# Gathering the lower expert outputs of a decoder layer in four groups, each behind one more down product

## The chip, the cores and the metric

One core of a Trainium2 chip runs the whole program. The metric is the device time of one execution in microseconds (us), median of several executions; less is better.

## What is computed

A decoder layer on x of shape 4 x 512 x 256 (2048 tokens): a Mamba mixer, cross attention over a context of 1601 positions, and a feed-forward part in which each token goes to two of eight experts. Only the last part is touched:

```python
scores = xt @ Wg.T
topk_scores, topk_idx = jax.lax.top_k(scores, TOP_K)          # TOP_K = 2
gate = jax.nn.silu(jnp.einsum('td,ehd->teh', xt, W1))
up = jnp.einsum('td,ehd->teh', xt, W2)
y = jnp.einsum('teh,edh->ted', gate * up, W3)
out = jnp.einsum('te,ted->td', w, y)                          # w: the two scores, zero elsewhere
return x + out
```

## The kernel before, in words

`decoder_kernel` calls `mixer_phase` (mixer and attention, everything up to about 731 us of the trace) and then `routed_ffn_phase`. All of the order there is written out by hand, engine by engine, with semaphores.

**Sorting.** The 4096 pairs of token and expert are sorted by expert, each expert's part padded to whole tiles of 128 rows. NT = 39 tiles are always computed, numbered 0 to 38; the last ones may be padding. GpSimd (POOL) gathers the token rows of all 39 tiles by indirect DMA (L1224).

**The tile loop.** For a tile, TensorE (PE) transposes the tokens (L1522), computes gate and up products (L1535), transposes the hidden rows (L1544, L1548) and computes the down product (L1559), whose last matmul raises `y_mm` by one: `y_mm` of n means that down products 0 to n - 1 are done. ScalarE (ACT) rounds tokens and hidden rows (L1266, L1277 to L1280) and does the silu (L1272). VectorE (DVE) takes the rests (L1427, L1435), multiplies (L1421), and copies the down product to SBUF (`evacuate`, L1442, the copy to `y_sb`). SyncE (SP) stores `y_sb` to `ffn_sorted` in DRAM (L1153, semaphores `y_st0` for even tiles and `y_st1` for odd ones) and fetches the tokens of the tile four ahead (L1148). PE, ACT and DVE run tiles two by two in a hardware loop, up to tile 36 of gate and up, and then a straight tail.

**Combining.** Each token has two result rows in `ffn_sorted`. The lower one belongs to the expert with the smaller number, so it is never in the last expert's tiles. POOL does, one after the other:

1. `stored(0)`: waits until all tiles of experts 0 to 6 are stored (L1245, L1206).
2. `fetch(y_one, 0, ...)`: 16 indirect gathers of 128 rows of 1 KB, the lower rows (L1239, semaphore `low_ld`).
3. It waits for all sixteen, and for the first 8 of the 16 groups of tokens multiplies by the score and adds to `x_all` (L1254, L1257).
4. `stored(1)`: waits until all tiles of all experts are stored.
5. `fetch(y_two, 1, ...)`: 16 gathers of the upper rows (L1239; `y_two` is part of the buffer `tok`), semaphore `up_ld[g // 2]` for each two.

DVE, in its tail, waits for `low_ld` behind the hidden rests of tile 38, adds the lower rows of the other 8 groups (L1477), copies the down product of tile 38, and then adds the upper rows for all 16 groups (L1487), each two as their gathers land. SP writes `out`, two groups at a time (L1176), waits for the last of it, and the program ends.

The small multiplications at L1206 (`take_wait`) only make POOL's waits take effect. The lines that the prediction speaks of are L1206, L1239, L1254, L1257, L1442, L1477, L1487 and L1176; those of POOL's second half:

```python
stored(0)
fetch(y_one, 0, lambda g: low_ld)
pool.wait_ge(low_ld, 16 * G)
...
stored(1)
fetch(y_two, 1, lambda g: up_ld[g // 2])
```

Of the kernel before, what the change touches and what calls it, by code (L numbers as in the profile page):

```python
# [20 lines left out]
def at(i, n=1):  # L21
    return bass.ds(i, n)
# [985 lines left out]
def routed_ffn_phase(nc, io, dims, env, sem, buf):  # L1008
# [5 lines left out]
    KD, G, KH, H_LAST, HH, NT = (env[k] for k in ("KD", "G", "KH", "H_LAST", "HH", "NT"))  # L1014
# [8 lines left out]
    with ExitStack() as ctx:  # L1023
        def sb(name, shape, dt=F32):
            return buf(ctx, name, shape, dt)
# [49 lines left out]
        y_one = sb("y_one", [P, G, D])  # L1075
        y_two = tok[:, 0:G, :]
# [29 lines left out]
        def so_far(i, p):  # L1106
# [3 lines left out]
        x_mm, xT_hi, xT_lo, gu_mm, silu2_ok, hid_ok, h_mm, hT_hi, hT_lo, y_mm, y_ok2 = (  # L1110
            sem(n) for n in ("x_mm", "xT_hi", "xT_lo", "gu_mm", "silu2_ok", "hid_ok", "h_mm", "hT_hi", "hT_lo", "y_mm",
                             "y_ok2"))
        low_ld, up_ld, comb = sem("low_ld"), [sem(f"up_ld{g}") for g in range(G // 2)], sem("comb")
# [14 lines left out]
        def gathered(i):  # L1128

            return 32 * (i // (2 * PAIRS) + 1) - (16 if i == NT - 1 and NT % 2 else 0)  # L1130

        def reload(eng, e, p, done):

            eng.wait_ge(w_ok, 2 * e + 2)
            load_expert(eng, e + 2, p, done)

        with nc.Block() as block:

            @block.sync
            def _(sp):  # L1140
                load_expert(sp, 0, 0, first_ld[0])
                load_expert(sp, 1, 1, first_ld[1])

                def load(i, q):

                    come = gathered(i) if isinstance(i, int) else (i - q) * (16 // PAIRS) + 32
                    sp.wait_ge(tok_ld[q // 2], come)
                    sp.dma_start(tok_in[:, q % 2, :], tok[:, at(i), :].rearrange("p a d -> p (a d)")  # L1148
                                 ).then_inc(tile_ld[q % 2], 16)

                def store(i, p):
                    sp.wait_ge(y_ok2, i + 1)
                    sp.dma_start(ffn_sorted[at(i * P, P), :], y_sb[:, p, :]).then_inc(y_st[p], 16)  # L1153

                for e in range(2):
                    reload(sp, e, e, first_ld[e])

                def store_and_load(i, q):


                    store(i, q % 2)
                    load(i + AHEAD, (q + AHEAD) % GROUP)

                GROUP = 2 * PAIRS
                LAST = (NT - AHEAD) // GROUP * GROUP
                with sp.Fori(0, LAST // GROUP) as j:
                    for q in range(GROUP):
                        store_and_load(GROUP * j + q, q)
                for i in range(LAST, NT - AHEAD):
                    store_and_load(i, i % GROUP)  # L1170
                for i in range(NT - AHEAD, NT):
                    store(i, i % 2)
                out = io["out"].rearrange("(g p) d -> p g d", p=P)
                for g in range(0, G, 2):
                    sp.wait_ge(comb, g + 2)
                    sp.dma_start(out[:, g:g + 2, :], x_all[:, g:g + 2, :]).then_inc(out_st, 16)  # L1176
                sp.wait_ge(out_st, 16 * (G // 2))

            @block.gpsimd
            def _(pool):  # L1180
                nc.gpsimd.iota(iot[:], pattern=[[1, P]], base=0, channel_multiplier=0).then_inc(iota_ok, 1)
                nc.gpsimd.iota(num[:], pattern=[[P, G]], base=0, channel_multiplier=1).then_inc(iota_ok, 1)
                nc.gpsimd.memset(tri[:], 1.0).then_inc(tri_zero, 1)
                nc.gpsimd.memset(ones[:], 1.0).then_inc(one_ok, 1)
                nc.gpsimd.memset(seg[:], 1.0).then_inc(one_ok, 1)
                pool.wait_ge(one_ok, 2)
                nc.gpsimd.memset(seg[:, :, 0:1], 0.0).then_inc(one_ok, 1)

                pool.wait_ge(tri_zero, 1)
                nc.gpsimd.affine_select(out=tri[:], in_=tri[:], compare_op=ALU.is_gt, fill=0.0, base=0,  # L1190
                                        pattern=[[1, P]], channel_multiplier=-1).then_inc(tri_ok, 1)
                def split(e, p):

                    for n, (lo, hi) in enumerate(PARTS):
                        nc.gpsimd.tensor_copy(w_hi[:, p * NW + lo:p * NW + hi], w_raw[:, p, lo:hi]).then_inc(hi_ok, 1)
                        pool.wait_ge(hi_ok, 2 * e + n + 1)
                        take_wait()
                        nc.gpsimd.tensor_tensor(w_lo[:, p * NW + lo:p * NW + hi], w_raw[:, p, lo:hi],
                                                w_hi[:, p * NW + lo:p * NW + hi].bitcast(F32), ALU.subtract).then_inc(w_ok, 1)

                taken = [0]

                def take_wait():

                    k = taken[0] % 16
                    nc.gpsimd.tensor_tensor(pool_scrap2[:, k:k + 1], ident[:, 0:1], ident[:, 0:1], ALU.mult)  # L1206
                    taken[0] += 1

                def next_expert(e, p, loaded, count):

                    last_tile = pool.value_load(tile_end[0:1, at(e - 2)], min_val=1, max_val=NT)
                    pool.wait_ge(y_mm, last_tile)
                    take_wait()
                    pool.wait_ge(loaded, count)
                    take_wait()
                    split(e, p)


                pool.wait_ge(id_ok, 1)
                for i in range(NT):  # L1220

                    if i % 2 == 0 and i >= 2 * PAIRS:
                        pool.wait_ge(tok_ld[i // 2 % PAIRS], gathered(i - 2 * PAIRS))
                    pool.indirect_dma_start(tok[:, i, :], None, xn3_dram,  # L1224
                                            bass.IndirectOffsetOnAxis(ap=tok_id[:, i:i + 1], axis=0)
                                            ).then_inc(tok_ld[i // 2 % PAIRS], 16)
                pool.wait_ge(tab_ok, 1)
                for p in range(2):
                    next_expert(2 + p, p, first_ld[p], 128)
                    reload(pool, 2 + p, p, wts_ld[p])  # L1230
                with pool.Fori(2, E // 2 - 1) as j:
                    for p in range(2):
                        next_expert(2 * j + p, p, wts_ld[p], 64 * (j - 1))
                        reload(pool, 2 * j + p, p, wts_ld[p])
                for p in range(2):
                    next_expert(E - 2 + p, p, wts_ld[p], 64 * (E // 2 - 2))
                def fetch(y, k, done):
                    for g in range(G):
                        pool.indirect_dma_start(y[:, g, :], None, ffn_sorted,  # L1239
                                                bass.IndirectOffsetOnAxis(ap=pos[:, k, g:g + 1], axis=0)).then_inc(done(g), 16)  # L1240

                def stored(n):

                    for p in range(2):
                        stores = pool.value_load(tile_end[0:1, E + 2 * p + n:E + 2 * p + n + 1], min_val=1, max_val=NT)  # L1245
                        pool.wait_ge(y_st[p], stores * 16)
                        take_wait()

                pool.wait_ge(pos_ok2, 1)
                stored(0)  # L1250
                fetch(y_one, 0, lambda g: low_ld)
                pool.wait_ge(low_ld, 16 * G)
                for g in range(BY_POOL):
                    nc.gpsimd.tensor_scalar(y_one[:, g, :], y_one[:, g, :], w_low[:, 0, g:g + 1], None,  # L1254
                                            ALU.mult).then_inc(low_part, 1)
                    pool.wait_ge(low_part, g + 1)
                    nc.gpsimd.tensor_tensor(x_all[:, g, :], x_all[:, g, :], y_one[:, g, :], ALU.add).then_inc(low_in, 1)  # L1257
                stored(1)
                fetch(y_two, 1, lambda g: up_ld[g // 2])

            @block.scalar
            def _(act):
# [376 lines left out]
```

## Time and profile before

| | us |
|---|---|
| median of three runs | 1065.64 |
| lowest and highest of them | 1062.32, 1066.44 |
| span of the profiled execution (first to last instruction) | 1119.2 |
| PE busy | 908.4 (81%) |
| DVE busy | 670.0 (60%) |
| POOL busy | 599.3 (54%) |
| ACT busy | 446.0 (40%) |

The three runs were timed without the profiler. The execution that the profiler recorded is another one, and its own time is known only as the span. An engine's busy time counts its data instructions alone. A row of the timeline gives the start, the duration, the engine, the line, the operation, and in brackets how long the engine sat idle before it and what ended that: a DMA, another engine's instruction, "issue" (nothing that the profile shows) or "remote" (a releaser that the profile does not know).

### The profile page before, as it was taken

The page shows a single profiled execution, that of the slowest core. Times are in us where ns is not written, and L with a number is a line of the kernel's source. Part 1 is how long each engine was busy: PE and PEld are TensorE (multiplying, and loading weights), DVE is VectorE, ACT ScalarE, POOL GpSimd, SP SyncE. Part 2 cuts the span into 40 slices and gives each one's busy share as a digit, 9 for nine tenths or more (in the row PEclk, how much of TensorE's full clock was granted, in tenths as well). Part 3 has the DMA queues.
Part 4 walks back from the last instruction along what each step waited for, and adds up shares of the span by engine and source line. Part 5 has one row for each costly group of instructions (what it writes and reads, how often), then busy time and mean ns, then how long its engine had stood idle before and what let it go on. Part 6 is the DMA issues. An engine that isn't in the chain of part 4 may idle for free. (4 is left out here: it accounts for less than half of the span.)

```text
span 1119.2 us, 16281 instructions
## 1 busy us (share of the span) xinstructions
PE 908.4 (81%) x5148; PEld 723.8 (65%) x5149; DVE 670.0 (60%) x1091; ACT 446.0 (40%) x827; POOL 599.3 (54%) x499
## 2 busy tenths in 40 slices
PE   5767667899969999788998779736279999999665
PEld 2344345576856677665677647735279999999564
DVE  5188789887789877876878433275034444443215
ACT  2555754467554476543555112231023333332111
POOL 2157785866666676658777132007743466425750
PEclk9989887999969999988999589957589999999686
DMA  9450020000170000530003100045513332212222
GB/s 321 157 199 1 2 113 38 1 15 1 40 264 1 16 1 2 199 103 7 9 1 110 42 7 8 20 155 191 146 39 115 115 115 75 78 37 70 61 89 90
DMA packets 48955, 85.45 MB, mean 76 GB/s; under 512 B 6292, under 2 KB 38696, under 8 KB 46856
## 3 DMA queue, kind: packets, MB, share of 16 engines
q1 hardware_dynamic: 43032, 65.77, 17.4%
q0 software_dynamic: 5872, 19.02, 5.6%
q8 instruction: 29, 0.48, 0.2%
q14 instruction: 22, 0.18, 0.1%
HBM read 65.64 MB, written 14.55 MB: 72 GB/s over the span
## 5 line engine op out<-in xcount | busy, mean ns | idle before, releaser
L413 POOL TENSOR_TENSOR u<-dtx,b_all 128x512 f32<-128x512 f32 x256 | 324.9, 1281 | 176.6 <-DVE h L662 172.9
L662 DVE TENSOR_TENSOR_SCAN h<-da,u 128x512 f32<-128x512 f32 x256 | 307.5, 1215 | 55.8 <-ACT da L497 33.9
L497 ACT ACTIVATE da<-dt_,a_neg 128x512 f32<-128x512 f32 x256 | 174.5, 690 | 105.9 <-DVE h L662 105.2
L785 PEld LDWEIGHTS ysum<-ident,h 128*128 128x128 f32 x1024 | 128.4, 152 | 94.5 <-DVE h L662 45.0
L785 PE MATMUL ysum<-ident,h 128*128 128x128 f32 x1024 | 157.7, 293 | 32.5 <-DVE h L662 25.5
L1421 DVE TENSOR_TENSOR hid<-act_,ps_u 128x352 f32<-128x352 f32 x78 | 40.4, 521 | 134.7 <-ACT act_ L1272 128.4
L965 PE MATMUL pv<-pT,ctx_n 128*128 128x128 f32 (+1 forms) x832 | 104.6, 276 | 1.4 <-DVE x_all L722 1.3
L965 PEld LDWEIGHTS pv<-pT,ctx_n 128*128 128x128 f32 (+1 forms) x832 | 98.4, 192 | 6.5 <-DVE x_all L722 3.2
L936 PE MATMUL pa<-ctx_t,xnT_a 128*128 128x401 f32 (+1 forms) x256 | 94.2, 502 | 3.6 <-ACT xnT_a L548 1.8
L1272 ACT ACTIVATE act_<-ps_g 128x352 f32<-128x352 f32 x78 | 36.1, 465 | 149.9 <-PE ps_u L1535 92.6
L1559 PE MATMUL ps_y<-w_hi,hidT_hi 128*128 x234 | 68.1, 291 | 19.0 <-issue 15.0
L1559 PE MATMUL ps_y<-w_hi,hidT_lo 128*128 x234 | 68.1, 291 | 15.2 <-issue 15.2
L1559 PE MATMUL ps_y<-w_lo,hidT_hi 128*128 x234 | 68.1, 291 | 13.1 <-issue 13.1
L768 PE MATMUL pm<-xnT_m,w_in 128*128 128x512 f32 x128 | 68.8, 645 | 10.2 <-DVE xs L619 5.3
L1206 POOL TENSOR_TENSOR pool_scrap<-ident 128x1 f32<-128x1 f32 x28 | 5.1, 192 | 121.8 <-PE ps_y L1559 103.5
L774 PE MATMUL pm<-xs,w_dt 128*128 128x512 f32 x128 | 65.8, 622 | 5.2 <-DVE xs L619 4.5
L1435 DVE TENSOR_TENSOR hidT_lo<-ps_h,hidT_hi 128x512 fp32r<-128x512 f32 (+2 forms) x117 | 42.1, 415 | 41.1 <-ACT hidT_hi L1277 29.6
L936 PEld LDWEIGHTS pa<-ctx_t,xnT_a 128*128 128x128 f32 x256 | 45.2, 190 | 33.0 <-DVE sim L645 4.8
L1277 ACT CAST hidT_hi<-ps_h 128x512 fp32r<-128x512 f32 x39 | 22.9, 587 | 102.7 <-PE ps_h L1548 82.0
L645 DVE COPY_PREDICATED sim<-mask,pa 128x401 f32<-128x401 uint8 x64 | 38.3, 600 | 42.4 <-PE pa L936 41.3
L1224 POOL DMA_INDIRECT tok<-xn_dram,tok_id x39 | 43.8, 1124 | 35.7 <-DVE tok_id L1403 24.2
L1559 PEld LDWEIGHTS ps_y<-w_hi,hidT_hi 128*128 128x128 f32 x234 | 46.2, 197 | 22.0 <-issue 22.0
(217 smaller groups left out, 1796.4 us busy)
## 6 DMA issues: line engine op xcount, KB each, us to landing
b_all<-b_dram SPq DMA_DIRECT2D x16, 1024.0 KB, 4.7
ctx_t<-in_ctxT SPq DMA_DIRECT2D x4, 1601.0 KB
ctx_n<-in_ctx SPq DMA_DIRECT2D x4, 1536.0 KB
ffn_sorted<-yg SPq DMA_DIRECT2D x1, 4992.0 KB, 22.5
ffn_sorted<-y_sb SPq DMA_DIRECT2D x39, 128.0 KB
tok_in<-tok SPq DMA_DIRECT2D x35, 128.0 KB
mask<-in_mask SPq DMA_DIRECT2D x16, 200.1 KB, 2.4
w_raw<-in_w1T SPq DMA_DIRECT2D x4, 704.0 KB
```

The costliest lines, as they stand in the source:

```text
L413: nc.gpsimd.tensor_tensor(u[:, i % 2, :], dtx[:, j % 2, :], b_all[:, n, :], ALU.mult).then_inc(u_ok, 1)
L497: nc.scalar.activation(da[i % DS][:], dt_[:, j % 2, :], ACT.Exp, scale=a_neg[:, j, n:n + 1]).then_inc(da_ok, 1)
L662: nc.vector.tensor_tensor_scan(h[:, i % HS, :], da[i % DS][:], u[:, i % 2, :], 0.0, ALU.mult, ALU.add).then_inc(scan_ok, 1)
L768: last = nc.tensor.matmul(bank[:], w_in[:, k, j * P:(j + 1) * P], xnT_m[:, k, :], start=k == 0, stop=k == KD - 1)
L774: last = nc.tensor.matmul(DT_BANKS[j][:], w_dt[:, k, j * P:(j + 1) * P], of_row(xs, b, k), start=k == 0, stop=k == KI - 1)
L785: last = nc.tensor.matmul(ysum[:, t * P:(t + 1) * P], h[:, i % HS, t * P:(t + 1) * P], ident[:], is_transpose=True, start=n == 0 and t == ...
L936: last = nc.tensor.matmul(pa[c % 2][:, 0:hi - lo], xnT_a[:, k, q * P:(q + 1) * P], ctx_t[:, k, lo:hi], start=k == 0, stop=k == KD - 1)
L965: last = nc.tensor.matmul(pv[:, k * P:(k + 1) * P], ctx_n[0:w, c, k * P:(k + 1) * P], pT[0:w, c, :], start=c == 0 and k == 0, stop=c == KC ...
L1224: pool.indirect_dma_start(tok[:, i, :], None, xn3_dram, bass.IndirectOffsetOnAxis(ap=tok_id[:, i:i + 1], axis=0)).then_inc(tok_ld[i // 2 % ...
L1421: nc.vector.tensor_tensor(hid[:, p, c * HH:(c + 1) * HH], act_[:, c * HH:(c + 1) * HH], ps_u[c][:, 0:HH], ALU.mult).then_inc(hid_ok, 1)
L1435: nc.vector.tensor_tensor(hidT_lo[0:rows_in, c:c + n, :], bank[0:rows_in, col:col + n * P].rearrange("p (c m) -> p c m", m=P), hidT_hi[0:r ...
L1559: last = nc.tensor.matmul(ps_y[:, 0:D], x[:, c, :], w[:, at(e % 2 * NW + (2 * NGU + c * D), D)], start=c == 0 and n == 0, stop=c == KH - 1 ...
```

## The change

Ahead of gathers 0, 4, 8 and 12 of the lower rows POOL now waits for one more down product: `y_mm` of at least 32, 33, 34 and 35. The upper gathers are issued as before. `stored(0)` stays ahead of the first.

```diff
-                def fetch(y, k, done):
+                def fetch(y, k, done, spread):
                     for g in range(G):
+                        if spread and g % 4 == 0:
+                            pool.wait_ge(y_mm, NT - 7 + g // 4)
                         pool.indirect_dma_start(y[:, g, :], None, ffn_sorted,
                                                 bass.IndirectOffsetOnAxis(ap=pos[:, k, g:g + 1], axis=0)).then_inc(done(g), 16)
...
-                fetch(y_one, 0, lambda g: low_ld)
+                fetch(y_one, 0, lambda g: low_ld, True)
...
-                fetch(y_two, 1, lambda g: up_ld[g // 2])
+                fetch(y_two, 1, lambda g: up_ld[g // 2], False)
```

POOL before, from the second half of `stored(0)` to the first multiplication (`y_one` receives the lower rows, `pos` has their places):

```order
L1206 TENSOR_TENSOR pool_scrap<-ident 128x1 [waits y_st0]
L1245 TENSOR_LOAD tile_end
L1245 ISA x2
L1246 REGISTER_ALU
L1206 TENSOR_TENSOR pool_scrap<-ident 128x1 [waits y_st1]
L1239 DMA y_one<-ffn_sorted,pos 128x256 x16
L1254 TENSOR_SCALAR y_one<-y_one,w_low 128x256 [waits low_ld]
```

The same place in the changed kernel:

```order
L1206 TENSOR_TENSOR pool_scrap<-ident 128x1 [waits y_st1]
L1241 DMA y_one<-ffn_sorted,pos 128x256 [waits y_mm]
L1241 DMA y_one<-ffn_sorted,pos 128x256 x3
L1241 DMA y_one<-ffn_sorted,pos 128x256 [waits y_mm]
L1241 DMA y_one<-ffn_sorted,pos 128x256 x3
L1241 DMA y_one<-ffn_sorted,pos 128x256 [waits y_mm]
L1241 DMA y_one<-ffn_sorted,pos 128x256 x3
L1241 DMA y_one<-ffn_sorted,pos 128x256 [waits y_mm]
L1241 DMA y_one<-ffn_sorted,pos 128x256 x3
L1256 TENSOR_SCALAR y_one<-y_one,w_low 128x256 [waits low_ld]
```

The run of sixteen gathers now has four waits on `y_mm` in it; no other instruction moved. What stands behind the lower rows' additions on POOL, in the changed kernel (`tok` is the buffer of the upper rows):

```order
L1256 TENSOR_SCALAR y_one<-y_one,w_low 128x256
L1259 TENSOR_TENSOR x_all<-x_all,y_one 128x256 [waits low_part]
L1247 TENSOR_LOAD tile_end
L1247 ISA x2
L1248 REGISTER_ALU
L1206 TENSOR_TENSOR pool_scrap<-ident 128x1 [waits y_st0]
L1247 TENSOR_LOAD tile_end
L1247 ISA x2
L1248 REGISTER_ALU
L1206 TENSOR_TENSOR pool_scrap<-ident 128x1 [waits y_st1]
L1241 DMA tok<-ffn_sorted,pos 128x256 x16
```

This is as before but for line numbers: the upper gathers stand behind all that POOL does with the lower rows.

## Rows read from the trace of the kernel before

**Rows 1.** The core's span and mean granted TensorE clock.

```profile
core 0: 1119.2 us, clock 0.887
```

**Rows 2.** Timeline of DVE, the copies of down products (start us, duration, instruction, idle before).

```profile
781.48 0.42 DVE L1442 COPY y_sb<-ps_y 128x256 f32<-128x256 f32 x1 [1.99 <-PE ps_y L1559]
...
827.39 0.42 DVE L1442 COPY y_sb<-ps_y 128x256 f32<-128x256 f32 x1 [1.26 <-PE ps_y L1559]
...
1014.67 0.42 DVE L1442 COPY y_sb<-ps_y 128x256 f32<-128x256 f32 x1 [1.25 <-PE ps_y L1559]
...
1028.54 0.42 DVE L1442 COPY y_sb<-ps_y 128x256 f32<-128x256 f32 x1 [1.25 <-PE ps_y L1559]
...
1059.35 0.42 DVE L1442 COPY y_sb<-ps_y 128x256 f32<-128x256 f32 x1 [1.25 <-PE ps_y L1559]
...
1066.27 0.42 DVE L1442 COPY y_sb<-ps_y 128x256 f32<-128x256 f32 x1 [1.25 <-PE ps_y L1559]
...
1073.13 0.42 DVE L1442 COPY y_sb<-ps_y 128x256 f32<-128x256 f32 x1 [1.25 <-PE ps_y L1559]
...
1103.32 0.42 DVE L1442 COPY y_sb<-ps_y 128x256 f32<-128x256 f32 x1 [1.13 <-PE ps_y L1559]
...
1109.89 0.42 DVE L1442 COPY y_sb<-ps_y 128x256 f32<-128x256 f32 x1 [1.05 <-PE ps_y L1559]
```

**Rows 3.** Timeline of POOL: last token gather, then the combining.

```profile
811.03 0.95 POOL L1224 DMA_INDIRECT tok<-xn_dram,tok_id  x1 [0.30 <-issue]
...
1024.04 0.19 POOL L1206 TENSOR_TENSOR pool_scrap<-ident 128x1 f32<-128x1 f32 x1 [8.89 <-DMA ffn_sorted<-y_sb]
...
1025.40 1.04 POOL L1239 DMA_INDIRECT y_one<-ffn_sorted,pos  x1 [0.52 <-issue]
1026.74 0.96 POOL L1239 DMA_INDIRECT y_one<-ffn_sorted,pos  x1 [0.30 <-issue]
...
1029.26 0.95 POOL L1239 DMA_INDIRECT y_one<-ffn_sorted,pos  x1 [0.30 <-issue]
...
1044.30 0.95 POOL L1239 DMA_INDIRECT y_one<-ffn_sorted,pos  x1 [0.30 <-issue]
1047.12 0.93 POOL L1254 TENSOR_SCALAR y_one<-y_one,w_low 128x256 f32<-128x256 f32 x1 [1.88 <-DMA y_one<-ffn_sorted,pos]
...
1060.18 0.74 POOL L1257 TENSOR_TENSOR x_all<-x_all,y_one 128x256 f32<-128x256 f32 x1
1068.48 0.19 POOL L1206 TENSOR_TENSOR pool_scrap<-ident 128x1 f32<-128x1 f32 x1 [7.56 <-DMA ffn_sorted<-y_sb]
...
1069.85 1.03 POOL L1239 DMA_INDIRECT tok<-ffn_sorted,pos  x1 [0.54 <-issue]
...
1088.75 0.95 POOL L1239 DMA_INDIRECT tok<-ffn_sorted,pos  x1 [0.30 <-issue]
```

**Rows 4.** Timeline of ACT around the long idle stretches.

```profile
816.12 0.46 ACT L1272 ACTIVATE act_<-ps_g 128x352 f32<-128x352 f32 x1 [25.61 <-remote]
...
1032.58 0.59 ACT L1277 CAST hidT_hi<-ps_h 128x512 fp32r<-128x512 f32 x1 [5.84 <-remote]
...
1034.10 0.37 ACT L1266 CAST tokT_hi<-ps_x 128x256 fp32r<-128x256 f32 x1 [0.62 <-remote]
1048.26 0.82 ACT L1272 ACTIVATE act_<-ps_g 128x352 f32<-128x352 f32 x2 [13.78 <-remote]
...
1092.70 0.82 ACT L1272 ACTIVATE act_<-ps_g 128x352 f32<-128x352 f32 x2 [13.82 <-remote]
```

**Rows 5.** Timeline of PE's weight loads in one such stretch.

```profile
1039.71 0.29 PEld L1559 LDWEIGHTS ps_y<-w_hi,hidT_lo 128*128 128x128 f32 x1 [1.13 <-issue]
```

**Rows 6.** Busy time by stretch: us, then PE, PEld, DVE, ACT, POOL; PEclk; DMA share; GB/s.

```profile
985.00:1028.00 43.00, 43.00 (x315) 42.87 (x314) 17.79 (x43) 12.83 (x37) 16.65 (x12) 1.00 0.12 40
1028.00:1049.00 21.00, 9.94 (x54) 8.53 (x52) 2.08 (x6) 2.02 (x6) 15.07 (x17) 0.73 0.36 106
```

**Rows 7.** Last piece of the chain that ended last: DVE's additions of upper rows.

```profile
1112.69 3.96 DVE x_all L1487 x10
```

## The prediction

> **What bounds the kernel now.** I read the span first [rows 1], then the copies of down products on DVE as a clock of the tile loop [rows 2], then POOL [rows 3], and then what ACT and PE did where the clock stopped [rows 4 to 6].
>
> The last copy is tile 38's (1109.89), the one ahead tile 37's (1103.32); tiles 36, 32 and 30 have no row here, so counting back, 1073.13 is tile 35, 1066.27 tile 34, 1059.35 tile 33, 1028.54 tile 31 and 1014.67 tile 29. Tiles 29 to 31 take 13.87 us, 6.93 us a tile, and in that stretch PE is busy for 43.00 of 43.00 us [rows 6]: the tile loop is TensorE's own speed. There are three places where it is not: tiles 0 to 2 take 45.91 us (781.48 to 827.39) where two tiles are 13.86, tiles 31 to 33 take 30.81, and tiles 35 to 37 take 30.19. They lose 32.0, 16.9 and 16.3 us. Each lies beside a long run of indirect gathers on POOL [rows 3]: the token gathers up to 811.98, the sixteen lower ones (1025.40 to 1045.25), the sixteen upper ones (1069.85 to 1089.70). ACT sits idle 25.61, 13.78 and 13.82 us for a releaser that the profile doesn't know, and goes on 4.1, 3.0 and 3.0 us after the last gather's issue [rows 3, 4]. PE issues one weight load in 1.4 us (1.13 idle plus 0.29) with "issue" ahead of it [rows 5], at a DMA share of only 0.36 [rows 6]. The clock falls to a mean of 0.73 there, between its two levels of 1.2 and 2.4 GHz, after PE had gone nearly idle.
>
> Read alone, this says: gathers stop the other engines, so spread them. But the timed runs say otherwise. The profiled span is 1119.2 us and the runs take 1065.64: **the recorded execution is at least 53.6 us longer than a timed one**, more if a time holds something around the span. The loop's other stretches run at PE's full speed and can't shrink by that. The three stalls can. So I take them for something that happens when the gathers' DMAs and the instructions are recorded together, and absent from the timed runs. The Trainium skill, page "NOTIFIC — the notification-queue block", section 7.1, says that a full internal pipeline of the recording block pushes back on whoever writes records and so can throttle an engine; the long span agrees with this, though no row names the block.
>
> **Before, with the stalls taken out (in the trace's time).** POOL's work is untouched by them, so its chain stands:
> - lower gathers from 1025.40, issued by 1045.25, POOL goes on at 1047.12 (1.87 us later), its eight multiplications and additions end at 1060.92, 13.80 us later [rows 3];
> - `stored(1)` needs tile 34 (it was released at 1068.48, 2.2 us after that tile's copy at 1066.27). Without stalls tile 34 is copied at 1028.54 + 3 x 6.93 = 1049.3, so the wait is over by 1051.5 and the upper gathers start straight behind the additions: 1060.92 + 1.37 (1068.48 to 1069.85) = 1062.3;
> - 19.85 us of issue and 1.87 to land: 1084.0; two last additions on DVE, 0.9 us (ten take 3.96 [rows 7], so 0.4 each); and from the last addition (1116.65) to the end of the span 2.55. **End: 1087.4.**
>
> PE's side ends sooner: tile 37 copied at 1028.54 + 6 x 6.93 = 1070.1, tile 38 6.6 us later at 1076.7 (1103.32 to 1109.89, an upper bound, as part of that was at the low clock), then 6.8 us of additions (1109.89 to 1116.65) and 2.55: 1086.1. POOL's chain bounds the end, by 1.3 us.
>
> A check on this: the tail shortens by 1119.2 - 1087.4 = 31.8 us and tiles 0 to 2 by 32.0, together 63.8. A span of 1055.4 is left, and 1065.64 - 1055.4 = 10.2 us of time around it. The Trainium skill, page "Runtime: NRT & Kernel Launch", section "The ~15µs preamble/postamble breakdown", gives some 9 to 15 us for what surrounds a kernel; no row here shows it.
>
> **The change, part by part.**
> - *Four waits.* They cost POOL nothing as instructions (the gap of 0.30 us between gathers already holds a register step). What counts is when they open. `y_mm` of 32 is tile 31, just ahead of its copy at 1028.5, 3 us after the first gather's present start, so already the first wait holds. The next open at 1035.4, 1042.3 and, for `y_mm` of 35 (tile 34), 1049.2. A group of four takes 4.81 us (1025.40 to 1029.26 + 0.95), less than a tile, so each group is done before the next wait opens.
> - *The last group* starts at 1049.2 + 0.3 = 1049.5, is issued by 1054.3, has landed by 1056.2. POOL's multiplications start then instead of at 1047.1: **+9.1 us**.
> - *Behind them* on POOL stand the additions (13.80), `stored(1)` and the upper gathers (19.85). Tile 34 is the very tile whose store `stored(1)` wants, and it is stored by 1051.5: the 9.1 us find no slack there, since in timed runs POOL never waited at `stored(1)`. The upper gathers go from 1062.3 to 1071.4, all else follows: end 1096.5, +9.1 us.
> - *DVE* wants `low_ld` for its own lower rows only behind tile 38's rests, about 1073: later than 1056, costs nothing. PE, ACT and SP wait for nothing that moved. PE's side still ends at 1086.1, now 10 us ahead of POOL's.
> - *What it gives back*: gathers and PE's work overlap less densely. Where no stall exists in timed runs, nothing. The bounds from the rows: 0, and all of the 16.9 us that tiles 31 to 33 lose. I take 0, because the time budget above closes without it.
>
> Sum: 1065.64 + 9.1 = **1074.7 us**. In the profiled execution the sum is a different one, since there the stalls are real (rival 1): I expect a recorded span of about 1110, below the 1119.2 of before, while the timed runs get slower.
>
> **Rivals.**
> 1. *The stalls are in every execution: faster.* ACT is held from about 9 us after a run of gathers begins (1034.5 after 1025.4), and idles 5.84 us already ahead of 1032.58 [rows 4]. Four gathers are over after 4.8 us, so a group would cost less than a third of 16.9; between 0 and 5.6 I take 2.5 for each of three: tile 34 at 1056.8 instead of 1066.27. POOL then: 5.1 + 1.9 + 13.8 + 1.4 after it, upper gathers 1079.0 to 1098.8, DVE held to 1101.8, some 14 additions (5.6) and 2.55: 1110.0, 9.2 us less than 1119.2, so 1056.4 us. With no cost per group it would be 17 less (1049), and if the upper gathers still catch tile 38, whose rests, product and 16 additions then follow their end, about 2 less. It decides if the timed runs hold at least about half of the recorded stalls. For it: all three stalls stand in the trace. Against it: the 53.6 us. The Trainium skill, page "Runtime: NRT & Kernel Launch", section "Instruction fetch mechanics", has each sequencer stream its instructions by DMA and stall at a branch whose target is not at hand; by it gathers could delay the fetches in every execution. The trace speaks half for it: "issue" ahead of PE's loads, but the second stall falls behind the loop's end, where nothing jumps back.
> 2. *A smaller stall in timed runs, mostly beside the upper gathers: no change.* PE's side is only 1.3 us from bounding the end before. If the upper gathers hold PE by h, before is longer by h - 1.3, while the changed kernel starts them at 1071.4, when PE has one tile left. From h of 5.1 the difference is under 5.3 us; at h = 10 it is 0.4 (1066). For it: the time around the span would be 10.2 - h, which no row forbids up to 10. Against: the same h beside the lower gathers delays tile 34 and adds to the 9.1.
> 3. *The lower groups hold PE a little each time: slower still.* Each of three groups with 2 us: tile 34 and so everything behind is 6 us later, +15, 1081.
> 4. *The waits are already met and nothing changes.* Only if POOL came to them late; it reaches them at 1025.4, 3 us ahead of the first and 24 us ahead of the last. Under 0.01.
>
> **How the numbers follow.** A measurement of this kernel can tell about 0.5%, 5.3 us, from no change. Forecast (+6 to +12) 0.65; rival 3 0.09; rival 2 0.15; rival 1 0.11. Faster by over 0.5%: 0.10; within 0.5%: 0.16 (rival 2 and a corner of 1); slower: 0.74. The range leaves out most of rival 1 below and the far part of rival 3 above: 1062 to 1081. The slower cases' own range is 1071 to 1081.
>
> **What would show it.** In the changed profile: gathers of `y_one` in four groups, each within 0.5 us behind a down product, the last behind tile 34's; POOL's multiplications 7.0 us behind that; `pool_scrap` behind the last addition without the 7.56 us of idle before; the upper gathers 22.2 us behind tile 34's down product; and still long idle stretches of ACT by the upper gathers. The stalls of tiles 31 to 33 should shrink in the recorded span, and the timed runs not gain by that. Wrong would be: timed runs at or below 1060, which would mean that the stalls are real, or timed runs unchanged, for which I would look for a hold of PE beside the upper gathers.

## The result, and the profile after

| | before | after |
|---|---|---|
| median of 14 runs each, us | 1065.61 | 1071.26 |
| lowest and highest, us | 1061.90, 1070.90 | 1069.07, 1079.43 |
| span of the execution profiled, us | 1119.2 | 1072.1 |
| that execution's own time, us | not known | 1073.92 |
| PE busy, us | 908.4 | 891.7 |
| POOL busy, us | 599.3 | 601.5 |

The ratio of the times is 1.0066 with a 95% interval of 1.0046 to 1.0086: the change costs 7.0 us (4.9 to 9.2), 9.1 forecast. (The ratio isn't that of the two medians, which differ by 5.7 us; the interval holds both.) The profiled span meanwhile fell by 47 us. Both are true, and the experiments show how. First the rows that answer to [rows 3], POOL's timeline in the changed kernel:

```profile
999.51 1.03 POOL L1241 DMA_INDIRECT y_one<-ffn_sorted,pos  x1 [3.79 <-PE ps_y L1561]
...
1006.51 0.94 POOL L1241 DMA_INDIRECT y_one<-ffn_sorted,pos  x1 [2.20 <-PE ps_y L1561]
...
1013.37 0.94 POOL L1241 DMA_INDIRECT y_one<-ffn_sorted,pos  x1 [2.16 <-PE ps_y L1561]
...
1020.38 0.94 POOL L1241 DMA_INDIRECT y_one<-ffn_sorted,pos  x1 [2.32 <-PE ps_y L1561]
...
1026.91 0.93 POOL L1256 TENSOR_SCALAR y_one<-y_one,w_low 128x256 f32<-128x256 f32 x1 [1.85 <-DMA y_one<-ffn_sorted,pos]
...
1040.95 0.19 POOL L1206 TENSOR_TENSOR pool_scrap<-ident 128x1 f32<-128x1 f32 x1 [0.24 <-issue]
...
1042.34 1.03 POOL L1241 DMA_INDIRECT tok<-ffn_sorted,pos  x1 [0.54 <-issue]
1043.67 3.19 POOL L1241 DMA_INDIRECT tok<-ffn_sorted,pos  x1 [0.30 <-issue]
...
1063.75 0.94 POOL L1241 DMA_INDIRECT tok<-ffn_sorted,pos  x1 [0.30 <-issue]
```

Four groups, each released by a down product; each group but the last is issued 2.2 us before the next one's wait opens. `pool_scrap` follows the last addition with no idle time: `stored(1)` has no slack to give. And DVE's copies, which answer to [rows 2]:

```profile
999.38 0.42 DVE L1444 COPY y_sb<-ps_y 128x256 f32<-128x256 f32 x1 [1.25 <-PE ps_y L1561]
...
1020.26 0.42 DVE L1444 COPY y_sb<-ps_y 128x256 f32<-128x256 f32 x1 [1.25 <-PE ps_y L1561]
...
1042.79 3.24 DVE L1479 SCALAR_TENSOR_TENSOR x_all<-y_one,w_low,x_all 128x256 f32<-128x256 f32 x8
1045.95 0.41 DVE L1444 COPY y_sb<-ps_y 128x256 f32<-128x256 f32 x1
...
1066.60 0.88 DVE L1489 SCALAR_TENSOR_TENSOR x_all<-tok,w_low,x_all 128x256 f32<-128x256 f32 x2 [1.59 <-DMA tok<-ffn_sorted,pos]
```

Tiles 31 to 34 (999.38 to 1020.26) take 20.88 us, 6.96 a tile: PE's own pace with four groups of gathers beside it. In the stretch of the gathers the windows view (window, its length, then busy us and count of PE, PEld, DVE, ACT and POOL, granted clock, DMA share, GB/s) shows no idle time on PE:

```profile
999.00:1026.00 27.00, 27.00 (x196) 26.92 (x196) 11.50 (x28) 8.42 (x24) 15.21 (x16) 1.00 0.40 114
```

No wait of ACT in the whole expert part has a releaser that the profile doesn't know. The long idles of [rows 4] aren't smaller here. They are absent.

### The profile page after: what moved, and what is told of

The parts are those of the page before. It is cut to its first block and busy times, and to the rows that moved or that the text cites. A ratio compares the mean times of both kernels' runs of the same rounds, so it can differ in the third digit from the quotient of the medians.

```text
span 1072.1 us, 16281 instructions
## 1 busy us (share of the span) xinstructions
PE 891.7 (83%) x5148; PEld 710.6 (66%) x5149; DVE 670.6 (63%) x1091; ACT 446.2 (42%) x827; POOL 601.5 (56%) x499
## 5 line engine op out<-in xcount | busy, mean ns | idle before, releaser
L785 PEld LDWEIGHTS ysum<-ident,h 128*128 128x128 f32 x1024 | 128.8, 152 | 95.8 <-DVE h L662 45.7
L1198 POOL TENSOR_TENSOR w_lo<-w_raw,w_hi 128x2816 fp32r<-128x2816 f32 (+1 forms) x12 | 58.6, 4884 | 0.0
L1537 PE MATMUL ps_g<-w_hi,tokT_hi 128*128 x156 | 54.3, 348 | 3.7 <-issue 3.7
```

The costliest lines, as they stand in the source:

```text
L785: last = nc.tensor.matmul(ysum[:, t * P:(t + 1) * P], h[:, i % HS, t * P:(t + 1) * P], ident[:], is_transpose=True, start=n == 0 and t == ...
L1537: last = nc.tensor.matmul(out[:, 0:HH], x[:, p, k * P:(k + 1) * P], w[:, at(e % 2 * NW + (first + k * HF), HH)], start=k == 0 and n == 0, ...
```

## Experiments

Places in different traces are given from the start of DVE's copy of tile 34's down product (1020.26 in the changed kernel). Ratios are to runs of the kernel before on the same chip.

### Before again, and where the last wait stands

The kernel before, unchanged:

> The kernel before, unchanged, for a second profile. Theory (the three long stalls of the recorded execution were no part of the timed runs): a profile of another execution can be without them; then tiles follow each other every 6.9 us all through, the span is some 2 us below the timed 1065.6, and POOL goes from its last lower addition to the upper gathers without a wait. Rival (the stalls are in every execution of before and the spreading removed them): the span is again near 1119, with three stretches of 14 to 26 us in which ACT idles.

Timed 1065.25 us, ratio 1.0002 (0.9986 to 1.0018). Its profiled execution took 1066.83 us with a span of 1065.0. The core's row, to be set against [rows 1]:

```profile
core 0: 1065.0 us, clock 0.907
```

The window of its sixteen lower gathers, where [rows 6] had the stall:

```profile
997.00:1018.00 21.00, 21.00 (x153) 20.91 (x152) 8.65 (x22) 6.32 (x18) 15.26 (x17) 1.00 0.44 131
```

PE is busy for all of the 21 us, with sixteen gathers in one run. **The same program, recorded in the same way, has no stall.** So recording alone doesn't make them. What this profile does give is the clean chain, on POOL,

```profile
1016.40 0.95 POOL L1239 DMA_INDIRECT y_one<-ffn_sorted,pos  x1 [0.30 <-issue]
1019.24 0.93 POOL L1254 TENSOR_SCALAR y_one<-y_one,w_low 128x256 f32<-128x256 f32 x1 [1.89 <-DMA y_one<-ffn_sorted,pos]
...
1034.67 1.03 POOL L1239 DMA_INDIRECT tok<-ffn_sorted,pos  x1 [0.54 <-issue]
...
1044.79 3.36 POOL L1239 DMA_INDIRECT tok<-ffn_sorted,pos  x1 [0.30 <-issue]
...
1056.56 1.04 POOL L1239 DMA_INDIRECT tok<-ffn_sorted,pos  x1 [0.30 <-issue]
```

and on DVE, the copy of tile 34 and the lower additions:

```profile
1021.56 0.42 DVE L1442 COPY y_sb<-ps_y 128x256 f32<-128x256 f32 x1 [1.24 <-PE ps_y L1559]
...
1044.09 3.24 DVE L1477 SCALAR_TENSOR_TENSOR x_all<-y_one,w_low,x_all 128x256 f32<-128x256 f32 x8
```

| place, us behind tile 34's copy | before again | changed | difference |
|---|---|---|---|
| POOL's first multiplication | -2.32 | 6.65 | 8.97 |
| first upper gather | 13.11 | 22.08 | 8.97 |
| last upper gather | 35.00 | 43.49 | 8.49 |
| end of span | 43.44 | 51.84 | 8.40 |

The shift goes down POOL's chain undiminished, and loses 0.5 us among the upper gathers. A gather whose issue lasts longer than its usual 0.95 us, as the 3.36 us above, is called held below.

Only the last of the four waits:

```diff
-                        if spread and g % 4 == 0:
-                            pool.wait_ge(y_mm, NT - 7 + g // 4)
+                        if spread and g == 12:
+                            pool.wait_ge(y_mm, NT - 4)
```

> Only the wait ahead of gather 12 stays (35 down products); gathers 0 to 11 go in one run as before. Theory (the price is the start of the last group, which delays POOL's multiplications and the upper gathers): the same time as the full change, ratio to before 1.0066, +7 us. Rival (the groups themselves cost or save something on PE): differs from the full change by more than 2 us; if the grouping hinders PE this one is faster, if it protects PE this one is slower.

1071.58 us, ratio 1.0065 (1.0046 to 1.0085), as the whole change. The first three waits cost nothing on such a chip, and spreading gives nothing, as far as these intervals tell (some 2 us).

All four waits one tile earlier:

```diff
-                            pool.wait_ge(y_mm, NT - 7 + g // 4)
+                            pool.wait_ge(y_mm, NT - 8 + g // 4)
```

> All four waits one down product earlier (31 to 34). Theory: the last group opens one tile, 6.9 us, sooner, so the multiplications start 2.2 us later than before instead of 9.1: ratio 1.000 to 1.003. Rival (any splitting of the gathers costs by itself, whatever the tile): stays near 1.0066.

1066.39 us, ratio 1.0019 (1.0005 to 1.0034), +2.0 us: 9.0 less one tile of 7.0. POOL multiplies 0.27 us ahead of the copy of tile 34:

```profile
1019.23 0.93 POOL L1256 TENSOR_SCALAR y_one<-y_one,w_low 128x256 f32<-128x256 f32 x1 [1.92 <-DMA y_one<-ffn_sorted,pos]
```

(tile 34's copy starts at 1019.50 in that trace).

And one tile later:

```diff
-                            pool.wait_ge(y_mm, NT - 7 + g // 4)
+                            pool.wait_ge(y_mm, NT - 6 + g // 4)
```

> All four waits one down product later (33 to 36). Theory: another 6.9 us on the chain, +14 to +16 us on before, ratio 1.013 to 1.015. Rival (the cost comes from something else than POOL's chain, for instance DVE waiting in its tail): less than +10 us.

1077.92 us, ratio 1.0124 (1.0103 to 1.0146), +13.2 us (11.0 to 15.5); 14 to 16 was expected. Earlier, as it was, and later make 2.0, about 7 and 13.2. In the traces POOL's first multiplication stands at -2.32 us from tile 34's copy before, then at -0.27, 6.65 and 13.56, and the end of the span at 43.4, 45.7, 51.8 and 58.7: the last wait's place sets the price, near one us for one us. No upper gather is held in this run, since DVE's lower additions are done when they begin. What is held instead is one of POOL's own additions:

```profile
1040.19 3.20 POOL L1259 TENSOR_TENSOR x_all<-x_all,y_one 128x256 f32<-128x256 f32 x1
```

Its neighbours take 0.73.

### Is it POOL's chain that sets the end?

If it is, the work between lower and upper gathers is worth its full length, until PE's side bounds. `BY_POOL` is the number of groups of tokens whose lower rows POOL adds; DVE adds the rest.

Kernel before, with none on POOL:

```diff
-        BY_POOL = G // 2
+        BY_POOL = 0
```

> The kernel before, with all 16 lower additions on DVE in its tail and none on POOL. Theory (the end is POOL's chain: lower gathers, eight additions of 13.8 us, upper gathers, and 7.2 us from the last gather's issue to POOL's end): the upper gathers start at the store of tile 34, some 9.5 us sooner; then DVE's side sets the end (16 + 16 additions behind tile 38's rests), 5 us less than before, ratio 0.995. Rival (PE's or DVE's tail bounds before already): DVE has 3.2 us more to do, so 0 to 3 us slower, ratio 1.000 to 1.003.

1059.14 us against 1064.56, ratio 0.9953 (0.9936 to 0.9969). POOL's timeline there ends with

```profile
1042.56 7.31 POOL L1239 DMA_INDIRECT tok<-ffn_sorted,pos  x1 [0.30 <-issue]
```

and DVE's at the same time is

```profile
1042.62 6.41 DVE L1477 SCALAR_TENSOR_TENSOR x_all<-y_one,w_low,x_all 128x256 f32<-128x256 f32 x16
1048.95 0.41 DVE L1442 COPY y_sb<-ps_y 128x256 f32<-128x256 f32 x1
1049.29 6.41 DVE L1487 SCALAR_TENSOR_TENSOR x_all<-tok,w_low,x_all 128x256 f32<-128x256 f32 x16
```

The last gather's issue lasts from the first of DVE's sixteen additions to 0.84 us behind their end. From there DVE bounds: all sixteen upper additions go in one piece.

Four groups on POOL, kernel before (`BY_POOL = 4`):

> The kernel before, with four lower additions on POOL (6.9 us) and twelve on DVE. Theory: POOL's side and DVE's side end together, 6 us less than before, ratio 0.994. Rival as for no additions on POOL: no gain.

1064.13 us, ratio 1.0012 (0.9995 to 1.0029): a miss, no gain. Two gathers lasted 5.45 and 5.57 us, beside two stretches of DVE's additions. The upper gathers start 6.35 us behind tile 34's copy, where it was 13.11 in before again, but the last of them at 34.35 where it was 35.00: of the 6.8 us saved, 6.1 are lost again among the gathers.

The changed kernel with none on POOL (`BY_POOL = 0`):

> The changed kernel (four groups behind 32 to 35 down products), with no addition on POOL. Theory: the late last group costs only because POOL's additions and the upper gathers stand behind it; without the additions the upper gathers start some 8.5 us behind tile 34's down product and DVE bounds the end, so it is within 1.5 us of the same kernel without the spreading (ratio 0.995 to 0.997). Rival (the spreading costs its 7 us by itself): 7 us above that kernel, ratio 1.002.

1066.92 us, ratio 1.0027 (1.0012 to 1.0042), 7.8 us above the same edit on the kernel before. It was to be within 1.5: I had reckoned that DVE's side hides the later gathers. Its POOL timeline,

```profile
1041.81 7.18 POOL L1241 DMA_INDIRECT tok<-ffn_sorted,pos  x1 [0.30 <-issue]
1049.29 4.77 POOL L1241 DMA_INDIRECT tok<-ffn_sorted,pos  x1 [0.30 <-issue]
```

and its DVE timeline:

```profile
1041.75 6.40 DVE L1479 SCALAR_TENSOR_TENSOR x_all<-y_one,w_low,x_all 128x256 f32<-128x256 f32 x16
...
1048.41 4.82 DVE L1489 SCALAR_TENSOR_TENSOR x_all<-tok,w_low,x_all 128x256 f32<-128x256 f32 x12
```

Two gathers take 11.95 us where two take 1.90. Shifted by the waits, the upper gathers lie across DVE's additions with four still to come, not with the last one. With nothing on POOL the kernel before holds only its very last gather, beside additions that have to be made anyway; here a second gather is held too, and three more stand behind it. From tile 34 to the end of the span it is 7.5 us more.

Two groups on POOL, kernel before (`BY_POOL = 2`):

> The kernel before, with two lower additions on POOL and fourteen on DVE. Theory: between the kernels with none and with four; DVE's side bounds, about 5.5 us less than before. Rival: no gain.

1058.32 us, ratio 0.9938 (0.9919 to 0.9956), and once more:

> The kernel with two lower additions on POOL and no spreading, once more. Theory (what pays depends on whether the chip stalls the engines beside a run of gathers): where before takes about 1120, the upper gathers already start right at the store of tile 34, so taking additions off POOL gains nothing, both stalls stay, and DVE's six more additions stand behind tile 38: 0 to 4 us slower than before, ratio 1.000 to 1.004. Where before takes about 1064: again 0.992 to 0.996. Rival (the gain is independent of the chip): 0.994 anywhere.

1058.99 against 1063.59, ratio 0.9953 (0.9926 to 0.9981). **This version beats the kernel before**, on the chip where both runs of it landed, by 5 to 7 us; the changed kernel wasn't run on that chip. It is nearly the same as none on POOL, so past this point POOL isn't the bound.

### Does DVE's addition hold the gather?

Two kernels were to tell, with DVE's additions of the lower rows left out (in both, those rows' part is missing from the output): the changed kernel with `BY_POOL = 0`, and the kernel before.

```diff
-                for g in range(BY_POOL, G):
-                    nc.vector.scalar_tensor_tensor(out=x_all[:, g, :], in0=y_one[:, g, :], scalar=w_low[:, 0, g:g + 1],
-                                                   in1=x_all[:, g, :], op0=ALU.mult, op1=ALU.add).then_inc(low_in2, 1)
...
-                    else:
-                        dve.wait_ge(low_in2, g - BY_POOL + 1)
```

> The spread kernel with no additions on POOL, and DVE's sixteen lower additions left out too (the lower experts' share is missing from the output). Theory: in the spread kernel without additions on POOL, one gather's issue took 7.2 us because it fell on DVE's run of sixteen additions; without that run it takes 0.95 us, the upper gathers end about 6 us sooner, and the time falls by at least 6 us, to a ratio of 0.996 or less. Rival (the long issue comes from the gathers' own queue or from a count of gathers): one gather still takes 5 us or more near the same place, and the time falls by 2 us at most.

> The kernel before with DVE's eight lower additions left out (half of the tokens lack the lower expert's share). Theory: the gather whose issue took 3.36 us in the second profile of before takes 0.95, and as POOL's last gather sets the end the time falls by about 2.4 us: ratio 0.997 to 0.999. If DVE's work itself bounded the end it would fall by 3.2 us or more. Rival (holds come from the queue): a gather above 3 us remains and the time is unchanged.

They ran on another chip, and there the kernel before takes 1120.10 us, in every one of 17 executions within 1115 to 1122. The first took 1107.08 us (ratio 0.9888, 0.9867 to 0.9908), the second 1119.03 (0.9996, 0.9985 to 1.0007). As a test of the hold they say nothing: PE stalls, and the places that were to be compared have moved apart. The upper gathers are over at 1080.21 and 1088.84, ahead of tile 37's copy (1089.62 and 1102.50), behind which the additions would have stood. So no run shows that the hold goes away with the additions.

What the traces do show is how it goes with their number, which `BY_POOL` sets. In ten traces, twice in two of them, a gather's issue is held by an unbroken run of DVE's additions:

| additions in the run | their time, us | the gather's issue, us | it ends behind the run by, us |
|---|---|---|---|
| 8 (five traces) | 3.24 | 3.07 to 4.13 | 0.82 to 0.84 |
| 12 (two) | 4.82 | 4.77, 5.45 | 0.82, 0.83 |
| 14 (three) | 5.61, 5.62 | 5.57, 6.49, 6.51 | 0.82, 0.83 |
| 16 (two) | 6.40, 6.41 | 7.18, 7.31 | 0.84 |

The run with two groups on POOL, as one of them:

```profile
1044.75 6.49 POOL L1239 DMA_INDIRECT tok<-ffn_sorted,pos  x1 [0.30 <-issue]
```

```profile
1044.81 5.61 DVE L1477 SCALAR_TENSOR_TENSOR x_all<-y_one,w_low,x_all 128x256 f32<-128x256 f32 x14
```

Wherever the issue begins, it ends 0.8 us behind the last addition. DVE isn't slowed: its eight take 3.24 us with a gather beside them and without (1105.60 in the first profile of before). There is an exception, though. In before again the second eight additions hold nothing, and neither do six in the run with the waits one tile earlier:

```profile
1048.32 3.25 DVE L1487 SCALAR_TENSOR_TENSOR x_all<-tok,w_low,x_all 128x256 f32<-128x256 f32 x8
```

```profile
1048.45 1.16 POOL L1239 DMA_INDIRECT tok<-ffn_sorted,pos  x1 [0.30 <-issue]
```

Why these let the gathers pass, no run tells.

The kernel before without its lower additions shows one thing more, ACT as in [rows 4]:

```profile
1047.55 0.82 ACT L1272 ACTIVATE act_<-ps_g 128x352 f32<-128x352 f32 x2 [13.85 <-remote]
...
1091.86 0.82 ACT L1272 ACTIVATE act_<-ps_g 128x352 f32<-128x352 f32 x2 [13.80 <-remote]
```

So the stalls aren't of an execution. They are of a chip, or of its condition, and there they cost time in every run. One rival is left: each of the 17 executions has a span (1113.6 to 1120.2 us) and a granted clock on record, so each was recorded, and whether such a chip also stalls when nothing is recorded wasn't tested.

### The change on a chip that stalls

The changed kernel itself, once more:

> The changed kernel itself, once more, because the last two runs met a chip on which the kernel before takes 1120 us in every execution, with the long stalls in its trace, while on two other chips it takes 1064 without them. Theory now (the stalls belong to the chip, and last as long as a run of gathers does): if this run meets a chip where before takes about 1120, the change is faster there, by 5 to 20 us (ratio 0.982 to 0.996), because the three groups ahead of tile 34 cost 1 to 3 us each instead of 17 together. If it meets one where before takes about 1064, the ratio is again 1.005 to 1.009. Rival (the price on POOL's chain is the same on every chip): ratio 1.006 wherever it runs.

It landed on a second chip of that kind: before 1120.61 us (1117.99 to 1121.42), changed 1104.84 (1103.31 to 1105.59), ratio 0.9862 (0.9841 to 0.9884). **There the same change is 15.5 us faster.** DVE's copies of tiles 31 to 37 (its other rows left out):

```profile
1026.80 0.42 DVE L1444 COPY y_sb<-ps_y 128x256 f32<-128x256 f32 x1 [1.25 <-PE ps_y L1561]
1033.81 0.42 DVE L1444 COPY y_sb<-ps_y 128x256 f32<-128x256 f32 x1
1042.23 0.42 DVE L1444 COPY y_sb<-ps_y 128x256 f32<-128x256 f32 x1 [0.94 <-PE ps_y L1561]
1049.77 0.42 DVE L1444 COPY y_sb<-ps_y 128x256 f32<-128x256 f32 x1 [0.34 <-PE ps_y L1561]
1057.43 0.42 DVE L1444 COPY y_sb<-ps_y 128x256 f32<-128x256 f32 x1 [0.52 <-PE ps_y L1561]
1064.42 0.42 DVE L1444 COPY y_sb<-ps_y 128x256 f32<-128x256 f32 x1 [1.14 <-PE ps_y L1561]
1071.06 0.42 DVE L1444 COPY y_sb<-ps_y 128x256 f32<-128x256 f32 x1 [1.13 <-PE ps_y L1561]
```

and the first two and the last upper gather on POOL, the second of them held by eight additions here too:

```profile
1071.95 1.03 POOL L1241 DMA_INDIRECT tok<-ffn_sorted,pos  x1 [0.54 <-issue]
1073.29 4.13 POOL L1241 DMA_INDIRECT tok<-ffn_sorted,pos  x1 [0.30 <-issue]
...
1093.99 0.94 POOL L1241 DMA_INDIRECT tok<-ffn_sorted,pos  x1 [0.30 <-issue]
```

Tiles 31 to 35 take 30.63 us where four take 27.7: the spread gathers cost PE 2.9 us in all, not 16.9. The upper gathers start behind tile 37, so their stall finds no tile but the last, and the 16.3 us of tiles 35 to 37 are gone as well. The copy of tile 37 stands 44.3 us behind that of tile 31, against 74.8 in [rows 2]. Of these 30 us half reach the end, for POOL's chain now bounds there too. The stall beside the token gathers, which the change doesn't touch, remains, as ACT's timeline shows:

```profile
803.30 0.46 ACT L1274 ACTIVATE act_<-ps_g 128x352 f32<-128x352 f32 x1 [18.62 <-remote]
815.26 0.46 ACT L1274 ACTIVATE act_<-ps_g 128x352 f32<-128x352 f32 x1 [11.50 <-remote]
```

## Why the prediction came out right, and where its steps were wrong

The path on which the forecast rests (last wait, multiplications, upper gathers, end) is the one that the runs show. The cause that it gave for the stalls and the level of its sum were wrong, and luck had a part in it.

**The tile loop is PE's own pace.** Right: 6.96 us a tile in both kernels where no stall is, PE busy throughout.

**The stalls are absent from the timed runs.** Right as a conclusion: 1119.2 against 1065.64 could mean nothing else. **Its cause is wrong.** I took the recording itself. Recording alone adds nothing of the kind: the same kernel before was recorded at a span of 1065.0 without any stall, while on two chips it takes 1120 in every one of 24 executions. The Trainium skill's rule on back-pressure (page "NOTIFIC — the notification-queue block", section 7.1) is borne out by no run here. The profile before is thus most likely one of a stalling chip, the timed runs beside it are of one that doesn't stall; on which chips either was taken isn't known to me. The chance of the forecast was in truth a chance on the kind of chip, which the text didn't see: that the changed kernel was then measured where nothing stalls was luck as far as the text knew, for on the other kind the time would have fallen.

**The last group starts at 1049.5 and POOL's multiplications move by 9.1 us.** Right, 8.97. The run with the last wait alone and the two that moved it by a tile confirm that it is this wait and no other. The other signs came too: multiplications 6.65 us and upper gathers 22.08 us behind tile 34's copy (7.0 and 22.2 behind its down product were given), and `pool_scrap` after 0.24 us of idle time.

**No slack behind it.** Right, the upper gathers moved by 8.97. At the end 8.4 us is left, since before again holds its upper gathers a little longer (3.36, 1.16, 1.21 and 1.07 us; 3.19, 1.02 and 1.19 in the changed kernel). Timed, 7.0 (4.9 to 9.2), which holds the 8.4 and the 9.1.

**Nothing is given back.** Right where the chip doesn't stall. On the others the change is 15.5 us faster instead of 7.0 slower, so there it gives back over 20 us. The reason given for the 0 was the time budget, and that budget didn't close: see the next step.

**The level of the sum.** Here two errors met. I worked out a clean span of 1055.4 and so 10.2 us around it. What lies around it is 1.8 us (1066.83 less 1065.0, 1073.92 less 1072.1), so the clean span of the runs is 1063.8. The Trainium skill, page "Runtime: NRT & Kernel Launch", section "The ~15µs preamble/postamble breakdown", gives some 9 to 15 us for what surrounds a kernel. These runs show 1.8 us as time less span, and the measurement decides. Before again, with its span of 1065.0, is 9.6 us above 1055.4, and three terms make that up to within 0.4 us: tiles 0 to 2 take 18.69 us, not 13.86 (4.8); the upper gathers take 22.93 us, not 19.85, mostly because one is held by DVE's additions (3.1); and from the last gather's issue to the end of the span it is 7.4 us, not the 5.3 of 1.87 + 0.9 + 2.55 (2.1). The last two are nearly the same in both kernels, and the first belongs to work that the change doesn't touch (15.06 us in the changed kernel's trace: it varies with the execution), which is why a difference could come out right from a level that was off. POOL also bounded the end by more than the 1.3 us given: without its additions the kernel gained 5.

**A recorded span near 1110, with long idles of ACT.** Wrong, 1072.1 and none, from the wrong cause above. On a stalling chip it is 1102.3.

**Rival 1, the stalls are in every execution.** Wrong on the chips of the comparison, right on two others, and its size too: it gave 9 to 17 us faster, 15.5 was measured. A group cost 0.7 us rather than 2.5. The page that stood beside it (the Trainium skill, "Runtime: NRT & Kernel Launch", "Instruction fetch mechanics") is neither shown nor refuted by that: no row names what holds the sequencers. The text also counted the stalls wrongly there: PE's hardware loop ends with the down product of tile 35, so it is the third stall (tiles 35 to 37) that falls behind the loop's end, and the second (tiles 31 to 33) falls inside it.

**Rivals 2 and 3, a smaller hold of PE in timed runs.** Out: PE was busy for 21.00 of 21.00 and 27.00 of 27.00 us beside the lower gathers, and the two tiles behind tile 35 take 6.75 and 6.64 us. **Rival 4**: the waits do hold, POOL idles 3.79, 2.20, 2.16 and 2.32 us at them.

What stays open is what makes a chip stall its engines beside a run of gathers. No run told that; nothing was varied on purpose but the kernel.

## What to carry to other kernels

When a profiled span and the timed runs differ by more than a few us, get a second profile of the same kernel, on another chip, before reasoning on either: here the two most likely describe different chips, and the sign of the change depends on which one it is measured on. A wait put on an engine is priced by when it opens and by whether anything behind it on that engine has slack; the last of several waits is the only one that counts, if the ones between are met in time. And look for a long run of VectorE additions beside GpSimd's DMA issues: moving either apart is worth microseconds, and a shift can move one onto the other.

## What the hardware did that was not expected

- **Chips differ.** The kernel before takes about 1064 us on two chips and 1120 on two others, all with the same program. On the slower ones PE and ACT nearly stop beside a run of sixteen gathers or more (ACT idles 13.85 and 13.80 us; in the first profile PE is busy for 9.94 of 21.00 us), and four gathers with a pause behind them cost 0.7 us.
- **DVE's additions hold POOL.** A gather's issue, alone 0.95 us, lasts until 0.8 us behind the end of DVE's run, 7.31 us at most, in twelve cases; a POOL addition of 0.73 us lasted 3.20. Two DVE operations of another kind do it too: in before again a token gather (760.24, 4.88 us) ends 0.83 us behind two subtractions of weights (759.55, 4.74 us). But not each stretch holds, as the second eight additions of before again showed. The Trainium skill, page "DMA: Bandwidth & Descriptors", section "SWDGE vs HWDGE vs iDMA", says that GpSimd writes its descriptors to rings in SBUF and is locked out of it while DVE is in its 2-port performance mode. The trace agrees in kind; in which mode these additions run no row shows.
- **The end comes late behind a gather.** 7.4 us pass from the end of the last gather's issue to the end of the span in every kernel that POOL bounds (1072.1 less 1064.69, 1065.0 less 1057.60, 1075.7 less 1068.26), though DVE's last addition ends 4.1 to 4.6 us ahead of it. Part of that stretch has a name. In the changed kernel SP's stores of `out` give

```profile
L1176 SPq DMA_DIRECT2D out<-x_all x8: 372/372/382, 1049.9 to 1067.5; - x8
DMA to landing us min/median/max: 2.1/2.3/2.7
```

so the last store is issued from 1067.5, right behind DVE's last addition (1067.48), and lands by about 1070, an estimate from these rows; the program waits for it. What fills the 2 us from there to 1072.1 no row names.
